# A masked-attention block with layer norm: sums leave PSUM as one product, the residual is added later from SBUF, and VectorE takes more of the last block's work

## The reference

```
scores = x @ ks.T
scores = leaky_relu(scores, negative_slope=0.2)
scores = where(adj > 0, scores, -9e15)
attn   = softmax(scores, axis=1)
y      = x + attn @ ks
out    = (y - mean(y)) / sqrt(var(y) + 1e-5)      # over the last axis
```

## Time and profile before

| | |
|---|---|
| median of 3 runs | 1552.41 us (1552.19 to 1553.93) |
| the profiled execution: time, span of its instructions | 1553.36 us, 1551.6 us |
| granted TensorE clock, mean | 0.996 of full speed |
| PE busy | 1502.5 us, 97% |
| DVE busy | 1502.6 us, 97% |
| ACT busy | 1475.7 us, 95% |
| POOL busy | 1440.9 us, 93% |
| DMA | 55.5% of 16 engines' time |

### The profile page before, as it was taken

How to read it: one execution, slowest core, us unless ns; L and a number is a source line. 1 busy time by engine, 2 the same in 40 slices (tenths; PEclk the granted TensorE clock), 3 DMA queues, 4 the chain that set the end, 5 groups by cost and what they waited for, 6 DMA issues and landing times.

```text
span 1551.6 us, 43289 instructions
## 1 busy us (share of the span) xinstructions
PE 1502.5 (97%) x16784; PEld 1414.1 (91%) x16784; DVE 1502.6 (97%) x1809; ACT 1475.7 (95%) x1883; POOL 1440.9 (93%) x1245
## 2 busy tenths in 40 slices
PE   5699999999999999999999999999999999999997
PEld 3499999999999999999999999999999999999987
DVE  7999999999999999999999999999999999999984
ACT  6799999999999999999999999999999999999997
POOL 4999999999999999999999999999999999999996
PEclk9999999999999999999999999999999999999999
DMA  9855556555555655555555555655555555555510
GB/s 350 278 194 190 198 197 202 198 188 194 194 192 190 203 190 192 194 192 194 202 191 191 188 187 188 201 183 188 193 190 188 200 182 191 194 188 190 196 63 8
DMA packets 107131, 296.00 MB, mean 191 GB/s; under 512 B 10800, under 2 KB 40240, under 8 KB 106928
## 3 DMA queue, kind: packets, MB, share of 16 engines
q1 hardware_dynamic: 106928, 293.25, 55.5%
HBM read 289.01 MB, written 4.19 MB: 189 GB/s over the span
## 4 chain that ended last, share of the span: by engine, by line
PE 76%; issue 9%; DVE 8%; ACT 5%; POOL 2%; DVEq 0%; DMA 0%; ACTq 0%; POOLq 0%
PE weighted L796 21%; PE scores L748 11%; PE scores L750 11%; PE scores L749 11%; PE weighted L812 7%; PE weighted L808 7%; PE weighted L810 7%; DVE running L654 3%; DVE ring L670 2%; ACT ring L491 2%; DVE ring L640 1%; ACT pt_hi L498 1%; POOL pt_lo L399 1%; ACT scores L484 1%; PE scores L796 0%
## 5 line engine op out<-in xcount | busy, mean ns | idle before, releaser
L394 POOL TENSOR_TENSOR ring<-ring,floor 128x768 f32<-128x768 f32 (+1 forms) x498 | 704.0, 1414 | 48.1 <-ACT floor L511 47.9
L399 POOL TENSOR_TENSOR pt_lo<-ring,pt_hi 128x512 f16<-128x512 f32 (+1 forms) x512 | 658.3, 1286 | 18.1 <-ACT pt_hi L498 17.3
L640 DVE SCALAR_TENSOR_TENSOR ring<-adj_sb,scores 128x1024 f32<-128x1024 int32 x512 | 621.2, 1213 | 6.0 <-ACT scores L484 5.6
L484 ACT ACTIVATE scores<-scores,shrink 128x1024 f32<-128x1024 f32 x512 | 553.6, 1081 | 51.4 <-PE scores L750 46.8
L491 ACT ACTIVATE ring<-ring,lift 128x1024 f32<-128x1024 f32 x512 | 583.6, 1140 | 5.3 <-DVE ring L670 4.0
L748 PE MATMUL scores<-xt_hi,kt_hi 128*128 128x256 f16 x2048 | 560.0, 273 | 25.9 <-DVE ring L640 17.6
L750 PE MATMUL scores<-xt_hi,kt_lo 128*128 128x256 f16 x2048 | 560.5, 274 | 0.0
L749 PE MATMUL scores<-xt_lo,kt_hi 128*128 128x256 f16 x2048 | 560.4, 274 | 0.0
L654 DVE TENSOR_TENSOR running<-ring,running 128x1024 f32<-128x1024 f32 x448 | 547.7, 1223 | 0.1
L796 PE MATMUL weighted<-k_rows,ring 128*128 128x129 f32 x3472 | 472.6, 276 | 2.0 <-DVE y L691 0.9
L796 PEld LDWEIGHTS weighted<-k_rows,ring 128*128 128x128 f32 x3472 | 427.6, 192 | 14.1 <-ACT ring L491 8.1
(11 more groups left out here) (74 smaller groups left out, 544.2 us busy)
## 6 DMA issues: line engine op xcount, KB each, us to landing
adj_sb<-in_adj SPq DMA_DIRECT2D x512, 512.0 KB, 3.4
ring<-in_ks_t SPq DMA_DIRECT2D x8, 512.0 KB, 7.2
x_row<-in_x SPq DMA_DIRECT2D x32, 128.0 KB, 3.5
out<-normed SPq DMA_DIRECT2D x32, 128.0 KB, 3.6
x_probe<-in_x_t SPq DMA_DIRECT2D x29, 128.0 KB, 3.5
xt_raw<-in_x_t SPq DMA_DIRECT2D x29, 128.0 KB, 4.6
ring<-in_ks SPq DMA_DIRECT2D x12, 128.0 KB, 4.8
k_rows<-in_ks SPq DMA_DIRECT2D x12, 128.0 KB, 4.6
```

Of the source, the lines that this page charges most:

```text
L394: nc.gpsimd.tensor_tensor(here, here, below, ALU.subtract).then_inc(gap_ready, 1)
L399: nc.gpsimd.tensor_tensor(pt_lo[:, g % PARTS, 0:QUAD - whole, :], ring[:, g % RING, whole:, :], pt_hi[:, g % PARTS, 0:QUAD - whole, :], AL ...
L640: nc.vector.scalar_tensor_tensor(ring[:, g % RING, :, :], adj_sb[:, g % ADJS, :, :], 0.0, scores[:, g % 2, :, :], ALU.is_le, ALU.subtract)\
```

## The change

1. `finish(b)` no longer scales the denominator. It takes the reciprocal straight from PSUM and multiplies both sides' sums by it in one instruction, into a new SBUF tile `ratio` (128 x 256). `ratio_ready` then lets TensorE overwrite `weighted`.
2. A new step `residual(b)` makes `y = ratio x unscale + x`, for each side. It reads `ratio` and `x_row`, both in SBUF. In blocks 0 to 30 it stands at the end of VectorE's slot, after the least; in the last block directly behind the finish.
3. In the slot of a finish, VectorE's gap of that slot is issued ahead of the finish instead of after the mask.
4. VectorE does all four tiles of the gap for the last 18 groups (14 before) and three tiles for the two ahead of these. The gap of the last block on VectorE waits for `spread_ready` (TensorE) instead of `floor_ready` (ScalarE's copy, which is not made for the last block now, as GpSimd has no gap there).
5. The high parts of the last 8 groups go from ScalarE to VectorE (`tensor_copy` from SBUF to SBUF).
6. The last block is normalised on VectorE, as `(y - mean) x rstd`, and GpSimd's `shift` is left out for it.

```diff
-    LEFT_OUT = GROUPS - 2
+    LEFT_OUT = GROUPS + 2
+    LAST_HIGHS = 8
...
-            return QUAD if g >= ALL - LEFT_OUT else 3 if g >= ALL - GROUPS else min(1 + g % 4, 2)
+            return QUAD if g >= ALL - LEFT_OUT else 3 if g >= ALL - LEFT_OUT - 2 else min(1 + g % 4, 2)
...
             def low_part(g):
-                pool.wait_ge(part_hi_ready, g + 1)
+                wait_high(pool, g)
...
-                dve.wait_ge(floor_ready, b + 1)
+                if b == BLOCKS - 1:
+                    dve.wait_ge(spread_ready, b + 1)
+                else:
+                    dve.wait_ge(floor_ready, b + 1)
...
             def finish(b):
-                at = b % 2
                 total = sums(b)[:, 0:SIDES * LANES].rearrange("p (j w) -> p j w", j=SIDES)
                 dve.wait_ge(weighted_ready, GROUPS * (b + 1))
-                nc.vector.tensor_scalar(denom[:, :], total[:, :, ONES], scale_rows, None, ALU.mult).then_inc(denom_ready, 1)
-                dve.wait_ge(denom_ready, b + 1)
+                wait(dve, ratio_ready, b)
+                nc.vector.reciprocal(recip[:, :], total[:, :, ONES]).then_inc(recip_ready, 1)
+                dve.wait_ge(recip_ready, b + 1)
                 wait(dve, y_ready, SIDES * b)
-                nc.vector.reciprocal(recip[:, :], denom[:, :]).then_inc(recip_ready, 1)
+                nc.vector.tensor_tensor(ratio[:, :, :], total[:, :, 0:D],
+                                        recip[:, :].unsqueeze(2).to_broadcast([P, SIDES, D]), ALU.mult)\
+                    .then_inc(ratio_ready, 1)
+
+            def residual(b):
+                at = b % 2
+                dve.wait_ge(ratio_ready, b + 1)
                 dve.wait_ge(xrow_loaded[at], 16 * (b // 2 + 1))
-                dve.wait_ge(recip_ready, b + 1)
                 wait(dve, normed_ready, SIDES * b)
                 for j in range(SIDES):
-                    nc.vector.scalar_tensor_tensor(y[:, j, :], total[:, j, 0:D], recip[:, j:j + 1],
-                                                   x_row[:, at, j, :], ALU.mult, ALU.add,
-                                                   accum_out=y_sum[:, j:j + 1]).then_inc(y_ready, 1)
+                    nc.vector.scalar_tensor_tensor(y[:, j, :], ratio[:, j, :], unscale_rows, x_row[:, at, j, :],
+                                                   ALU.mult, ALU.add, accum_out=y_sum[:, j:j + 1]).then_inc(y_ready, 1)
+
+            def high_part(g):
+                dve.wait_ge(prob_ready, g + 1)
+                dve.wait_ge(weighted_ready, g + 1 - PARTS)
+                whole = WHOLE[g % GROUPS]
+                nc.vector.tensor_copy(pt_hi[:, g % PARTS, 0:QUAD - whole, :], ring[:, g % RING, whole:, :])\
+                    .then_inc(dve_hi_ready, 1)
+
+            def normalise(b):
+                dve.wait_ge(normed_ready, SIDES * b)
+                dve.wait_ge(out_stored[b % 2], 16 * (b // 2))
+                dve.wait_ge(rstd_ready, b + 1)
+                for j in range(SIDES):
+                    nc.vector.tensor_scalar(normed[:, b % 2, j, :], y[:, j, :], neg_mean[:, j:j + 1], rstd[:, j:j + 1],
+                                            ALU.add, ALU.mult).then_inc(normed_ready, 1)
 
             for s in SLOTS:
-                b = whole(s, AT_FINISH)
-                if b is not None:
-                    finish(b)
+                ended = whole(s, AT_FINISH)
+                if ended is not None:
+                    if ended < BLOCKS - 1:
+                        gap(s - AT_GAP + 1)
+                    finish(ended)
+                    if ended == BLOCKS - 1:
+                        residual(ended)
                 g = group(s, 0)
                 if g is not None:
                     mask(g)
+                g = group(s, AT_PART)
+                if g is not None and g >= ALL - LAST_HIGHS:
+                    high_part(g)
+                if whole(s, AT_NORMALISE[0]) == BLOCKS - 1:
+                    normalise(BLOCKS - 1)
...
-                    if g is not None and early == (g % GROUPS > 0):
+                    if g is not None and early == (g % GROUPS > 0) and (ended is None or ended == BLOCKS - 1):
                         gap(g)
...
+                if ended is not None and ended < BLOCKS - 1:
+                    residual(ended)
...
                 if q == 0 and b < BLOCKS - 1:
-                    wait(pe, y_ready, SIDES * b)
+                    wait(pe, ratio_ready, b)
```

More of the change, by code:

```diff
@@ L172, in adj_attention_layernorm @@
         dve_gap_ready = sem("dve_gap_ready")
+        dve_hi_ready = sem("dve_hi_ready")
         part_hi_ready = sem("part_hi_ready")
         part_lo_ready = sem("part_lo_ready")
-        denom_ready = sem("denom_ready")
+        ratio_ready = sem("ratio_ready")
         prob_ready = sem("prob_ready")
@@ L225, in adj_attention_layernorm @@
         scale_rows = f32_column(scale, K_ALL)
+        unscale_rows = f32_column(unscale, K_ALL)
         def scales_there(stage):
@@ L265, in dve_tiles, with wait_high @@
         def dve_tiles(g):
-            return QUAD if g >= ALL - LEFT_OUT else 3 if g >= ALL - GROUPS else min(1 + g % 4, 2)
+            return QUAD if g >= ALL - LEFT_OUT else 3 if g >= ALL - LEFT_OUT - 2 else min(1 + g % 4, 2)
+        def wait_high(eng, g):
+            if g < ALL - LAST_HIGHS:
+                eng.wait_ge(part_hi_ready, g + 1)
+            else:
+                eng.wait_ge(dve_hi_ready, g + 1 - (ALL - LAST_HIGHS))
         @block.sync
@@ L527, in _ @@
                 g = group(s, AT_PART)
-                if g is not None:
+                if g is not None and g < ALL - LAST_HIGHS:
                     high_part(g)
@@ L550, in _ @@
                         bound_x(b)
-                b = whole_late(s, AT_SPREAD, 1)
-                if b is not None:
+                b = whole(s, AT_SPREAD)
+                if b is not None and b < BLOCKS - 1:
                     spread(b)
@@ L695, in _ @@
-            for s in SLOTS:
-                b = whole(s, AT_FINISH)
-                if b is not None:
-                    finish(b)
+                    nc.vector.scalar_tensor_tensor(y[:, j, :], ratio[:, j, :], unscale_rows, x_row[:, at, j, :],
[6 more added lines that the diff above has]
+                    .then_inc(dve_hi_ready, 1)
```

5 lines of the change are left out of this document (3 added, 2 removed).

## The result

| | before | after |
|---|---|---|
| median of 14 runs each | 1553.44 us (1551.72 to 1553.93) | 1555.75 us (1554.68 to 1557.05) |
| ratio of the two, 95% interval | | 1.0017 (1.001 to 1.0024) |
| the profiled execution: time, span | 1553.36, 1551.6 us | 1554.68, 1552.9 us |
| DVE / PE busy | 1502.6 / 1502.5 us | 1522.8 / 1499.2 us |
| ACT / POOL busy | 1475.7 / 1440.9 us | 1468.8 / 1443.4 us |

The change costs 2.3 us, 0.17%. The forecast was 1556.5. (The profiled execution of the changed kernel is the shortest of its 14, so the two traces differ by 1.3 only.) Behind the small number stand two larger ones: the steady part became some 6 us slower, the end some 4 us faster.

A forecast was written before the change was run, and what follows sets the result against it. TensorE and VectorE were taken as nearly equal bounds, needing 46.29 and 46.24 of 46.48 us per block. Steady part +7.5 and end -3.4 gave 1557.5 from the profiled 1553.36, 1556.5 from the median 1552.41; 8-in-10 range 1545.5 to 1559.5.

The forecast's parts named there:

- the likeliest case: Whole kernel: GpSimd holds VectorE's first least in the steady blocks, the end gets shorter; 1556.5 us, chance 0.60.
- the likeliest single outcome: Whole kernel: measured slower than before by more than about 0.2% (3.1 us), chance 0.48.
- first exponential of the last block: End, ScalarE: no longer behind the copy of the floor, this exponential was placed by hand 1.1 us earlier.
- The late mean and the hold: Steady blocks: later y delays GpSimd's mean, so its low part overlaps VectorE's first least by 0.50, costing 0.36 us.
- The residual unheld: Steady blocks: GpSimd is done with its low part and waiting on the mean, so the residual costs VectorE nothing extra.
- residual held as well: Rival, steady blocks: residual meets GpSimd's low part; half of 1.16 us in each of 30 blocks, 1573, chance 0.06.
- VectorE's added work: Steady blocks, around the finish: new sum 1.16 us against 1.07, so VectorE pays 0.09 more per block.
- no hold: Rival, steady blocks: GpSimd catches up or shared access lets both through; period 46.35 to 46.38, 1546.2 us, chance 0.24.
- TensorE's own need: Steady blocks: TensorE needs 46.29 us per block, the period of 46.48 less its stall of 0.19.
- TensorE's stall: Steady blocks: the 0.19 us wait for y before the first weigh of a block was to go.
- The end: Last groups through final normalisation: shorter by 3.4 us in sum, of which 3.0 up to the last finish.
- the rival that had the larger gain at the end: Hold in the blocks, but casts short and unheld (-4.4) and TensorE's clock staying up (-1): 1553.9 us, chance 0.10.

The follow-up runs named there:

- p_no_pow: Changed kernel with GpSimd's power replaced by a product, so rows are not normalised rightly: 1543.68 us against 1552.89 for the kernel before, ratio 0.9941.
- d_deviation_late: Changed kernel with GpSimd's deviation moved from five to thirteen slots after the finish, normalisation and store behind it: 1547.08 us against 1552.89 before, ratio 0.9964.
- a_residual_early: Changed kernel with the residual directly behind the product in every block: 1590.34 us against 1552.89 for the kernel before, ratio 1.0241.
- e_scaled_ones: Kernel before with the changed kernel's end and the column of ones multiplied by the scale once at the start: 1542.16 us against 1552.89, ratio 0.9932.
- b_steady_only: Changed kernel with the end of the kernel before: 1559.31 us against 1553.28 for the kernel before, ratio 1.0044.
- h_mean_late: Changed kernel with GpSimd's mean one slot later, so GpSimd does not wait for y: 1607.1 us against 1553.28 for the kernel before, ratio 1.035.
- i_ones_only: Kernel before, its end untouched, with the column of ones multiplied by the scale once on GpSimd at the start: 1545.69 us against 1552.79, ratio 0.9946.

## Why the prediction was right

It came out 0.7 us from the measured time, by the likeliest case and its mechanism. Part of that closeness is luck. The forecast was counted from 1552.41, the median of three runs; over 14 runs the same kernel has 1553.44. As a difference, 4.1 us were forecast and 2.3 measured, so that the likeliest single outcome, slower by more than 0.2%, did not come. Both halves erred to the same side: the steady part was forecast too slow, and the end gained more than forecast.

| step | predicted | measured |
|---|---|---|
| VectorE's own need of a block | 46.33 (+0.09) | 46.24 (0.00 to +0.02) |
| hold of the first least | 0.36 | 0.37, overlap 0.51 less 0.14 |
| distance of two finishes | 46.69 | 46.61 |
| blocks with a scale table, more than before | 0.8 each | 0.69 each |
| steady part | +7.5 | +5.3 in the trace, +6.0 alone on the chip |
| first exponential of the last block | -1.1 | -1.5 |
| ninth exponential | -2.3 | -2.8 |
| last finish | -3.0, and 0.15 | -4.0 |
| after the last finish | -0.25 | -0.29 |
| end | -3.4 | -4.3 in the trace, -3.9 alone on the chip |

- **The late mean and the hold** stood as worked out, to 0.02 us, and `p_no_pow` and `d_deviation_late` show the cause by taking it away in two ways. The margin was a difference of two sums of 33 us; from the second y's start GpSimd's low part was to end after 33.29 and the least to start after 32.79, and in the block shown they do so after 33.31 and 32.80.
- **The residual unheld** was right, and for the reason given. The step came with more room than forecast (0.25 or more, where 0.05 was worked out). The rival "residual held as well", priced at half a hold of 1.16 per block, at 1573, was too cheap: `a_residual_early` has two holds in every block and 1590.
- **VectorE's added work was mis-sized.** The reciprocal to its reader was priced at 0.27 as the earlier trace rows have it to y; from the reciprocal to the product it is 0.19, and the finish costs 1.09, not 1.16. Over 28 blocks that is 2.0 us, nearly the whole error of the steady part. With the smaller end, and with the 0.5 of the power behind the last finish, it is also why the rival "no hold" stood at 1546.2, where `p_no_pow` gives 1543.7. The count of distances was off as well: 29 lie between the finishes up to block 29, not 30, and 26 of them agree within 0.01, not 27.
- **TensorE's own need** was put at 46.29 and is 46.23 (`e_scaled_ones`), since the first product behind its stall gives way 0.06 later. It changed nothing here, as VectorE sets the pace.
- **TensorE's stall** was expected to go, and this was one of the prediction's own signs of being right. It stayed at 0.31, since a VectorE that is late by its hold is also late with the product. It cost nothing, as VectorE sets the pace; in `p_no_pow`, where the hold is gone, the stall is gone too.
- **The end** was under-sized by 0.9. The casts were taken to be long and unheld (0.68); they are short (0.48) and five of the eight are unheld. They brought 1.1, where 0.7 was in the sum; another 0.5 of the miss came ahead of them. 0.4 of that is there by the first exponential. It is an error of placing that exponential by hand and not the clock's, since in the kernel before the exponential starts at 1510.94 and the clock still reads 1.00 up to 1514. From the first to the ninth, the forecast struck 1.2 of waiting for TensorE off the 16.1, and 1.3 went. But the reason seems to be another: that wait is there in the traces in which the clock falls and gone in the others, `b_steady_only` with its old end among them, so it goes with the clock and not with TensorE being earlier. It also shows what was wrong with the rival that had the larger gain at the end. Short casts and the clock up both came true, but the 1.0 for the clock seems to have been in the forecast's 1.2 already, and the rival's 6.0 for the end (its own terms add up to 5.8) met 4.3.

For the cast the Trainium skill (VectorE: DVE Perf Modes, "The perf-mode tier table") gave twice the rate of a plain fp32 instruction. The trace agrees: from 512 to 768 elements the cast grows by 0.13 (0.48 to 0.61), while the subtraction grows by 0.27 from 256 to 512 (0.41 to 0.68). The estimate of 0.4 from it was short of the 0.48.

## What to carry to other kernels

When a step of VectorE with two SBUF operands is added or moved, lay GpSimd's timeline beside it and ask what GpSimd is doing at that time, and what it will be doing a whole block later if its own input now comes late. A wait of GpSimd can be what keeps VectorE free: `h_mean_late` lost 51 us by removing one. Where the aim is to release a PSUM tile sooner, first look for work that can leave the path altogether, like a scale folded into a constant (`i_ones_only`, -7.1 us), before splitting the path in two.

## What the runs showed of the hardware

- **The exclusion between VectorE and GpSimd works both ways and by whole instructions.** A VectorE instruction with SBUF operands only that starts while GpSimd runs ends late by the overlap less 0.14 to 0.20 (least: 0.51, +0.37; first y of `a_residual_early`: 0.80, +0.60; last cast: 0.98, +0.79), so an overlap of 0.2 costs nothing. GpSimd's gap that started during the held least was 0.25 longer for an overlap of 0.39, and the one at 347.05 was 1.08 longer for 1.23. The rule that the two exclude each other for whole instructions is in the Trainium skill (SBUF — State Buffer, "Who interferes with whom"), and the trace agrees.
- **Small instructions are mostly not spared, and two in a row can be held twice.** Three elements per partition took 1.22 instead of 0.28 (the mean of the three such instructions in `d_deviation_late`); a held first y of 128 elements took 0.73 to 1.66 instead of 0.35, and the second y 1.23 where GpSimd's next instruction stood ready (`a_residual_early`, `h_mean_late`), as that one starts before the first y has ended. Where GpSimd had to wait for y instead (`d_deviation_late`), the second y took 0.34. Instructions on a single element per partition were not held: four of them, from 343.57 to 344.16 in the changed kernel, took 0.14 to 0.15 each beside a GpSimd gap that ran from 342.99 to 344.27.
- **Operands in PSUM protect.** The 64 y of the kernel before, which read their sum from PSUM, have a mean of 349 ns beside a GpSimd gap of 1.27. The 64 of `a_residual_early`, with the same width and both inputs in SBUF, have 1027 ns beside a gap of the same size, and those of `h_mean_late` 1346 ns beside one of 1.82.
- **A cast from fp32 to fp16, SBUF to SBUF,** took 0.48 for 512 elements and 0.61 for 768 when not held. It has one input and was held by GpSimd all the same (0.94, 0.96, 1.40).
